# Cross-attention stack on one Trainium2 core: V weight splits, the narrow V and the first head's rows moved in the order of the projection stage

## What is computed

```python
q = x @ Wq; k = ctx @ Wk; v = ctx @ Wv          # 16 heads of 64
logits = einsum('qd,kd->qk', q, k) / 8 + col_bias   # a mask value at 4 named keys
out = softmax(logits) @ v
x = x + concat_heads(out) @ Wo + bo
```

## Time and profile before

| | |
|---|---|
| median of 3 runs | 4579.02 us |
| the profiled execution | 4576.37 us |
| its span, first to last instruction | 4574.6 us |
| granted PE clock, mean | 0.988 of 2.4 GHz |
| PE / DVE / POOL / ACT busy | 98% / 67% / 62% / 50% |
| DMA moved | 349.68 MB, mean 76 GB/s |

### The profile page before, as it was taken

One profiled execution on the slowest core, in us unless ns is written; L12 is line 12 of the kernel. 1 busy time (PEld: TensorE's weight loads), 2 busy tenths in 40 slices (PEclk: granted clock), 3 DMA queues, 4 the chain that ended last, 5 costly groups with the idle time before them and its releaser, 6 DMA issues.

```text
span 4574.6 us, 56775 instructions
## 1 busy us (share of the span) xinstructions
PE 4481.5 (98%) x20609; PEld 2828.0 (62%) x20609; DVE 3081.8 (67%) x5037; ACT 2308.6 (50%) x4121; POOL 2825.7 (62%) x1365
## 2 busy tenths in 40 slices
PE   8999999999999979999999999999999999999999
PEld 7888765656566445555556566656656666666664
DVE  4221567777777678777846777777766677777776
ACT  3232554555455436666655554545555545555553
POOL 0000388889888701011136898889875888898886
PEclk9999999999999979999999999999999999999999
DMA  5474921222221021111243222222126212222220
GB/s 189 156 221 150 305 68 38 66 66 69 48 64 48 13 41 15 13 14 16 57 133 92 64 69 47 66 64 64 41 50 219 63 45 60 63 69 61 51 48 30
DMA packets 124633, 349.68 MB, mean 76 GB/s; under 512 B 28085, under 2 KB 46005, under 8 KB 113338
## 3 DMA queue, kind: packets, MB, share of 16 engines
q1 hardware_dynamic: 124352, 346.04, 28.6%
HBM read 191.31 MB, written 120.31 MB: 68 GB/s over the span
## 4 chain that ended last, share of the span: by engine, by line
PE 93%; DVE 5%; issue 1%; DMA 1%; ACT 0%; SPq 0%; DVEq 0%; ACTq 0%
PE ST L1005 14%; PE SS L986 12%; PE ST L1006 12%; PE OA L1016 12%; PE OB L1016 11%; PE ST L1150 5%; PE OA L1158 4%; PE SS L1136 3%; DVE acc L1612 2%; PE OB L1136 1%; PE SS L1025 1%; PE ST L1081 1%; PE ST L1082 1%; PE ST L1083 1%; PE SS L1052 1%
## 5 line engine op out<-in xcount | busy, mean ns | idle before, releaser
L882 POOL TENSOR_TENSOR acc<-acc,P 128x1024 f32<-128x1024 f32 x912 | 2216.9, 2463 | 298.4 <-DVE acc L1618 285.3
L1346 ACT ACTIVATE P<-ST 128x512 f32<-128x512 f32 (+1 forms) x2496 | 1464.6, 598 | 1254.2 <-PE ST L1006 1128.6
L1591 DVE TENSOR_REDUCE mpart<-SS 128x1 f32<-128x400 f32 (+1 forms) x3072 | 1629.5, 570 | 666.4 <-PE SS L986 590.7
L1005 PE MATMUL ST<-QX,KX 128*128 128x512 f32 (+1 forms) x2496 | 1022.9, 410 | 2.3 <-ACT stw L1244 2.0
L986 PE MATMUL SS<-KS,QS 68*128 68x400 f32 (+1 forms) x3072 | 977.2, 352 | 13.6 <-DMA QS<-stq 8.0
L1006 PE MATMUL ST<-QS,KS 69*128 69x512 f32 (+1 forms) x2496 | 988.4, 396 | 0.0
L986 PEld LDWEIGHTS SS<-KS,QS 68*128 68x128 f32 x3072 | 583.6, 190 | 189.8 <-DVE xacc L1642 24.9
L1005 PEld LDWEIGHTS ST<-QX,KX 128*128 128x128 f32 (+1 forms) x2496 | 463.0, 186 | 359.5 <-issue 271.2
L1016 PE MATMUL OA<-P,Vp 128*64 128x512 f32 (+1 forms) x2496 | 658.3, 606 | 0.0
L1016 PE MATMUL OB<-P,Vp 128*64 128x512 f32 (+1 forms) x2496 | 641.3, 592 | 0.0
L1445 ACT ACTIVATE PG<-ST 128x512 f32<-128x512 f32 (+1 forms) x832 | 426.5, 616 | 215.6 <-PE ST L1150 215.5
(11 more groups left out here) (247 smaller groups left out, 4457.1 us busy)
## 6 DMA issues: line engine op xcount, KB each, us to landing
q_parts<-stq SPq DMA_DIRECT2D x96, 512.0 KB, 5.2
QX<-q_parts SPq DMA_DIRECT2D x96, 512.0 KB, 11.3
KX<-k_parts SPq DMA_DIRECT2D x48, 801.0 KB, 9.4
QS<-q_parts SPq DMA_DIRECT2D x45, 512.0 KB
R<-R SPq DMA_DIRECT2D x360, 64.0 KB, 2.0
v_tiles<-sv SPq DMA_DIRECT2D x24, 832.0 KB, 5.9
Vp<-v_tiles SPq DMA_DIRECT2D x24, 832.0 KB, 7.2
k_parts<-skh SPq DMA_DIRECT2D x48, 400.5 KB, 4.8
```

The costliest lines, as they stand in the source:

```text
L882: gp.tensor_tensor(out, out, P[0:k, slot(H, t), q, :], ALU.add).then_inc(pool_a, 1)
L1005: pe.matmul(bank, KX[H % 2][:, t * 128:t * 128 + k], QX[H % 2][:, q], start=True, stop=False)
L1346: act.activation(P[0:k, slot(H, t), j, :], ST[n % 3][0:k, :], ACT.Exp, scale=SCALE).then_inc(act_p, 1)
L1591: dve.tensor_reduce(mpart[H % 2][:, i // len(KCH), c:c + 1], SS[RING_AT["s", H, i] % 3][:, 0:w], AX.X, ALU.max).then_inc(dve_ss, 1)
```

## The change

Three parts. (1) ACT and DVE split the V weights of an iteration ahead of `take_k` in place of behind `split_wk`; the splits 2 and 3 of the start stand between the two halves of `take_k(0)`. (2) The thirteen transposes of the narrow V (`g`) and their ACT copies go behind the first quad's V, in the bank order too. (3) In SP's last K iteration the first head's K, key rows and bias rows are issued ahead of the last K stores, once PE is through with the last projection, and the four Q copies right behind these stores; the Wq stores, the waits for the landings and the rest of the Q phase follow.

```diff
--- before.py
+++ after.py
@@ -180,9 +180,11 @@
 def before_order():
 
     out = [("c", t, 0) for t in range(KT)]
-    out += [("k", 0, c) for c in range(4)] + [("g", i, 0) for i in range(4)]
+    out += [("k", 0, c) for c in range(4)]
     for qd in range(QUADS):
         out += [("v", qd, t) for t in range(KT)]
+        if qd == 0:
+            out += [("g", i, 0) for i in range(4)]
         if qd == X_QUAD:
             out += [("x", i, 0) for i in range(QT // 2)]
         out += [("k", 1 + 4 * qd + i, c) for i in range(4) for c in range(4)]
@@ -572,6 +574,21 @@
                     sp.wait_ge(dve_wk, m + 3)
                     load_wk(m + 4)
 
+            def load_head_k(H):
+                b, n = H % 3, H // 2
+                sp.dma_start(words(KS[b][0:D, :]), dK[n, H % 2, 0, :, :]).then_inc(d_s[b], 16)
+                sp.dma_start(words(KS[b][D:D + NROWS, :]), dExt[H // HEADS, :, :]).then_inc(d_s[b], 16)
+
+            def load_head_b(H):
+                sp.dma_start(words(QS[H % 3][D:SROWS, :]), dBias.rearrange("m r q -> (m r) q")).then_inc(d_s[H % 3], 16)
+
+            def copy_first_q(l):
+                H0 = l * HEADS
+                for q in range(JQ):
+                    sp.wait_ge(act_qh, QITEMS * l + q + 1)
+                    sp.dma_start(words(QS[H0 % 3][0:D, q * 512:q * 512 + 512]), words(stq[q][0:D, 1, :]))\
+                        .then_inc(d_s[H0 % 3], 16)
+
             store_k(0)
             next_wk(0)
             for qd in range(QUADS):
@@ -586,9 +603,18 @@
                 for w in range(4):
                     sp.dma_start(dV[4 * qd + w, :, :, :], sv[:, w, :, :]).then_inc(d_sv, 16)
                 for i in range(4):
-                    store_k(1 + 4 * qd + i)
-                    next_wk(1 + 4 * qd + i)
                     u, n = 4 * qd + 4 + i, 4 * qd + i
+                    if n + 1 == BIG * PAIRS:
+                        sp.wait_ge(pe_k, 4 * NW)
+                        sp.wait_ge(d_k[1], k_stored(1))
+                        sp.wait_ge(d_ext, 32)
+                        sp.wait_ge(d_bias, 32)
+                        load_head_k(0)
+                        load_head_b(0)
+                    store_k(1 + n)
+                    next_wk(1 + n)
+                    if n + 1 == BIG * PAIRS:
+                        copy_first_q(0)
                     if u + 2 < BIG * PAIRS:
                         sp.wait_ge(dve_wv, u + 1)
                         load_wv(u + 2)
@@ -609,14 +635,6 @@
             for b in range(2):
                 sp.wait_ge(d_wqo[b], 32 * (BIG * PAIRS // 2))
 
-            def load_head_k(H):
-                b, n = H % 3, H // 2
-                sp.dma_start(words(KS[b][0:D, :]), dK[n, H % 2, 0, :, :]).then_inc(d_s[b], 16)
-                sp.dma_start(words(KS[b][D:D + NROWS, :]), dExt[H // HEADS, :, :]).then_inc(d_s[b], 16)
-
-            def load_head_b(H):
-                sp.dma_start(words(QS[H % 3][D:SROWS, :]), dBias.rearrange("m r q -> (m r) q")).then_inc(d_s[H % 3], 16)
-
             def load_head_kx(H):
                 sp.dma_start(words(KX[H % 2][:, :]), dK[H // 2, H % 2, :, :, :].rearrange("r d k -> (r d) k"))\
                     .then_inc(d_x[H % 2], 16)
@@ -656,16 +674,11 @@
 
             def q_phase(l):
                 H0, n0 = l * HEADS, l * PAIRS
-                if l == 0:
-                    load_head_k(0)
-                    load_head_b(0)
                 if l == 2:
                     sp.wait_ge(pe_z, z_banks(H0))
                     load_wq(l, 1)
-                for q in range(JQ):
-                    sp.wait_ge(act_qh, QITEMS * l + q + 1)
-                    sp.dma_start(words(QS[H0 % 3][0:D, q * 512:q * 512 + 512]), words(stq[q][0:D, 1, :]))\
-                        .then_inc(d_s[H0 % 3], 16)
+                if l > 0:
+                    copy_first_q(l)
                 for q in range(QITEMS):
                     n = QITEMS * l + q
                     sp.wait_ge(pool_ql, n + 1)
@@ -952,15 +965,17 @@
                         last = pe.matmul(bank, wkl[b][:, ct, :], ch[:, ct, k], start=False, stop=ct == CCT - 1)
                     last.then_inc(pe_k, 1)
 
+            def transpose_vt():
+                pe.wait_ge(act_k, 4)
+                for i in range(4):
+                    at = BEFORE_AT["g", i, 0]
+                    wait_bank(pe, at)
+                    for t in range(4 * i, min(4 * i + 4, KT)):
+                        k, c = rows_of(t), (t - 4 * i) * 128
+                        last = pe.transpose(PB[at % 8][0:k, c:c + 128], vt[:, t * 128:t * 128 + k], ident[:, :])
+                    last.then_inc(pe_g, 1)
+
             project_k(0)
-            pe.wait_ge(act_k, 4)
-            for i in range(4):
-                at = BEFORE_AT["g", i, 0]
-                wait_bank(pe, at)
-                for t in range(4 * i, min(4 * i + 4, KT)):
-                    k, c = rows_of(t), (t - 4 * i) * 128
-                    last = pe.transpose(PB[at % 8][0:k, c:c + 128], vt[:, t * 128:t * 128 + k], ident[:, :])
-                last.then_inc(pe_g, 1)
             for qd in range(QUADS):
                 pe.wait_ge(dve_wv, 4 * qd + 4)
                 for t in range(KT):
@@ -972,6 +987,8 @@
                         pe.matmul(bank, ch[:, ct, k], wvl[:, ct, :, :], start=False, stop=False)
                         last = pe.matmul(bank, cl[:, ct, k], wvh[:, ct, :, :], start=False, stop=ct == CCT - 1)
                     last.then_inc(pe_v, 1)
+                if qd == 0:
+                    transpose_vt()
                 if qd == X_QUAD:
                     transpose_x()
                 for i in range(4):
@@ -1286,8 +1303,9 @@
                 wait(act, d_wqo[n % 2], 32 * (n // 2))
                 copy(wqs_h[n % 2][:, :, :], wq_raw[n % 2][:, :, :]).then_inc(act_wq, 1)
 
-            def take_k(m):
-                for c, (o, w) in enumerate(KCH):
+            def take_k(m, chunks=range(4)):
+                for c in chunks:
+                    o, w = KCH[c]
                     act.wait_ge(pe_k, 4 * m + c + 1)
                     bank = PB[BEFORE_AT["k", m, c] % 8]
                     if m == 0:
@@ -1299,17 +1317,21 @@
             split_group()
             for u in range(2):
                 split_wv(u)
-            take_k(0)
-            for m in range(2):
-                split_wk(m + 1)
-                split_wv(m + 2)
-            for i in range(4):
-                act.wait_ge(pe_g, i + 1)
-                c = min(4, KT - 4 * i)
-                k = rows_of(4 * i + c - 1)
-                copy(Vg[0:k, 4 * i:4 * i + c, :].rearrange("k t (g d) -> k (t g) d", g=GROUPS)[:, :, 0:D1],
-                     PB[BEFORE_AT["g", i, 0] % 8][0:k, 0:c * 128]
-                     .rearrange("k (t d) -> k t d", d=QD)[:, :, D1:2 * D1]).then_inc(act_g, 1)
+            take_k(0, range(2))
+            for u in range(2, 4):
+                split_wv(u)
+            take_k(0, range(2, 4))
+            for m in range(1, 3):
+                split_wk(m)
+            def take_vg():
+                for i in range(4):
+                    act.wait_ge(pe_g, i + 1)
+                    c = min(4, KT - 4 * i)
+                    k = rows_of(4 * i + c - 1)
+                    copy(Vg[0:k, 4 * i:4 * i + c, :].rearrange("k t (g d) -> k (t g) d", g=GROUPS)[:, :, 0:D1],
+                         PB[BEFORE_AT["g", i, 0] % 8][0:k, 0:c * 128]
+                         .rearrange("k (t d) -> k t d", d=QD)[:, :, D1:2 * D1]).then_inc(act_g, 1)
+
             act.wait_ge(pool_sv, 1)
             for qd in range(QUADS):
                 wait(act, d_sv, 64 * qd)
@@ -1318,15 +1340,17 @@
                     act.wait_ge(pe_v, KT * qd + t + 1)
                     copy(sv[0:k, :, t, :], PB[BEFORE_AT["v", qd, t] % 8][0:k, :].rearrange("k (w d) -> k w d", w=4))\
                         .then_inc(act_v, 1)
+                if qd == 0:
+                    take_vg()
                 if qd == X_QUAD:
                     take_x()
                 for i in range(4):
                     m, u, n = 1 + 4 * qd + i, 4 * qd + 4 + i, 4 * qd + i
+                    if u < BIG * PAIRS:
+                        split_wv(u)
                     take_k(m)
                     if m + 2 < NW:
                         split_wk(m + 2)
-                    if u < BIG * PAIRS:
-                        split_wv(u)
                     split_wq(n)
                     if qd == QUADS - 1:
                         split_x(0, i)
```

## The result

The changed kernel takes 4552.95 us (median of 6 runs, 4547.35 to 4556.11) against 4580.01 (6 runs, 4573.39 to 4583.03): a ratio of 0.9941, interval 0.9929 to 0.9954. The profiled execution took 4553.21, its span is 4551.4, 23.2 us less than before. The forecast was 4557 with a range from 4551 to 4562.

A forecast was written before the change was run, and what follows sets the result against it. The matrix engine, busy nearly the whole span, was taken as the bound, leaving idle and slow-clock time. 18.0 + 2.7 + 1.5 = 22.2 us off 4576.37 gives 4554.2 profiled, median 4556.8, rounded 4557; range 4551 to 4562.

The forecast's parts named there:

- The boundaries: At five K-to-V quad boundaries, earlier V splits remove the wait for narrow V weights: 18.0 us, low end 13.0.
- The narrow V: At the start, V begins 4.2 us earlier, less about 1.5 for thirteen transposes moved behind the first quad: net 2.7 us.
- The condition on the splits: At the start, V splits 2 and 3 must end before 28.3; if not, 1.4 us lost, bounds 1.3 and 2.8.
- The head part in front: Before the first score tile, Q copies land 3.2 us earlier at 121 GB/s; the 8.0 us stall shrinks to about 4.9.
- the bound of 6.0: Before the first score tile, going by SP's issue times alone, the restart comes 6.0 us earlier.
- What takes it back: Before the first score product, a new wait of about 1.5 us for the maxima row; head part nets 1.5 us.
- The risk of half clock: Behind the new maxima-row wait, at the first score product, some risk of half clock; 1.5 to 2.4 us if it came.
- Fast copies: Rival: Q copies fast in a full queue, store stream 3 us earlier, head part 4.7 to 7.1, median 4551 to 4554; chance 0.2.
- The kept stall: Rival: V still waits about 1 us at the boundaries, 18.0 becomes 8 to 13, median 4561 to 4567; chance 0.08.
- the slower case: Rival: late V loads stall ScalarE and some 16 K iterations, 2 us each at 15 us landing, 4607; chance 0.02.

The follow-up runs named there:

- e1: Kernel before plus the V split order alone (start and iterations), narrow V and SP as before: 4556.38 us, ratio 0.9952.
- e2: Kernel before plus only the thirteen narrow-V transposes moved behind the first quad's V: 4581.78 us, ratio 1.0006.
- e4: Kernel before with the four Q copies made twice, all eight waited for: 4581.47 us, one run.
- e5: Changed kernel with the four Q copies made twice behind the last K stores, all eight waited for: 4552.39 us, one run.
- e3: Kernel before plus SP's new order alone: 4575.09 us, ratio 0.9992.
- e9: The changed kernel run again, unaltered: 4552.61 us, ratio 0.9948; its profiled execution took 4561.14.
- e7: Changed kernel with head 0's maxima row issued by ScalarE on its own DMA queue: 4546.36 us, one run.
- e8: Changed kernel with the 2 MB of split Wq loaded one K iteration later: 4556.35 us, one run.
- e11: Changed kernel with head 0's maxima row on ScalarE's queue, timed: 4549.78 us, ratio 0.9939.
- e12: Changed kernel with the four Q copies and head 0's maxima row issued on ScalarE's queue: 4551.38 us, ratio 0.9942.

## Why the prediction was right, point by point

**The boundaries.** Forecast 18.0 us (4.2 three times, 2.7 twice); measured 4.30, 4.12, 2.71, 4.25, 2.72, together 18.10, and e1 alone shows it. V starts 0.18 us behind K at full clock, as taken from the passage to the Q product. The possible 1 or 2 us of ScalarE standing at the moved V load were there, 14.8 us in ten waits over the stage, longest 2.5, and the matrix engine waited for nothing behind them. The 18.0 was read from one execution; in e2 the same boundaries cost 16.7.

**The narrow V.** Forecast 2.7, measured 2.89 in the ledger; the transposes take 1.33 us (64.90 to 66.23) where I had 1.5. The condition on the splits was in the forecast, with its own bounds. What I did not work out is how much of the 2.7 belongs to the split order: e2 alone loses 3 us, and e1 wins 1.6 more than the five boundaries, so the moved transposes add only 1.3.

**The head part in front.** The step "the copies move at 121 GB/s, 0.52 MB in 4.3 us" failed: four more copies cost 2.2 to 2.9 us (e4, e5). Against the last K matmul the restart came 3.4 us earlier in e3 and 4.2 and 5.4 in the two profiles of the changed kernel, in place of 3.2: between my value and the bound of 6.0. The stall left was 2.8 us (4.0 in e3), not 4.9. The half clock behind it, which I took as unchanged, cost 3.4 us in place of 2.5. I had read a rate from a window in which the issues, not the transfers, may have been the limit.

**What takes it back.** The wait for the maxima row was forecast at 1.5 us and was 2.6. The row's landing, forecast about 2 us earlier against the end of K, was 0.9 us earlier in the first profile (66.1 against 67.0) and 2.0 in e9. The mechanism is the one described: it lies in the queue (e7), it comes with the SP order (e3), and since the row's landing stays at 66.1 to 66.2 us behind the last K matmul, it grows when the matrix engine reaches the row sooner (e8) and shrinks when it gets there later (e5). The risk of half clock behind it came true in e3 (1.7 us) and e8, and not in the changed kernel. The net of this part is 1.5 us against e1, 0.9 against before and 0.9 in e3, where 1.5 was booked. That it came out near is luck in part: two terms were off against each other, and the net is about as large as the scatter of K to P, 1.1 us in the changed kernel.

**What was missed.** The first Q product's bank wait (0.8 us, 0.9 in the ledger). ScalarE's wait for a K store behind the 2 MB of Wq was 3.2 us before, without effect; in the first profile it was 6.0, and the first Q product had to wait. e8 shows that the Wq load makes it. Much of the rise is scatter: the same kernel shows 4.1 us and no bank wait in e9, and kernels with the old SP order show 4.2 to 4.4 (e1, e2, e4). Why it lands that late in some executions was not tested.

**The rivals.** "Fast copies" was right in part for the copies and wrong in its result, since the stream behind did not come 3 us earlier. The measured median does lie in that rival's 4551 to 4554 and outside the 4555 to 4558.5 given to the forecast, but the marks show the forecast's mechanism and not the rival's. The kept stall and the slower case did not come. Of the 4 us that the median lies under the point, 1.0 is in the profiled execution (0.6 us less won than forecast at the first score product, 1.6 more behind it, cause not shown). About 3 come from the step to the medians: the profiled execution before lay 2.65 us under the median of its runs, and the one after lies 0.3 over its own, which is scatter.

## What to carry to other kernels

A low part that gates a big stage belongs ahead of the take-overs of results, when nothing waits for these but buffers: reordering two engines' lists won 19.7 us with no instruction changed. Before moving a load to the front of a full queue, look at the last thing in that queue with no slack, here an 8 KB row; here another queue brought it 4 us sooner. And two moves can be worth 2.9 us together where the second alone costs 3.

## What the runs showed of the hardware

The same idle time has no fixed price. Gaps of 2.4 us cost 0.1 or 1.5 us more. A wait of 2.5 us for the maxima row brought the half clock in e3, and one of 2.6 did not in the changed kernel. In e9 a wait of 1.12 us in the last layer came with 0.50, and one of 1.02 in the same place of the first profile with 1.00. Over the whole kernel this made 8 us between two executions of the same program. Small work in a gap may matter: in e2 an idle gap of 4.0 us at the start brought the half clock for 3 us, where the clock stayed at 1.00 in the three profiles with transposes in that gap. The Trainium skill, "TensorE: Matmul & The Clock Gate", Part 1, says that the monitor is free-running against the kernel; these pairs of like waits with a different clock agree with it.

An 8 KB row needed 9.2 us to land behind SP's stores (9.25 in e9) and 5.0 us from ScalarE's queue (4.8 in e11) under the same load. In e12 the issues of the first two copies on that queue took 0.5 us each and those of the next two 2.6 and 2.3, in which ScalarE stood still for 2.0 and 1.3 us. The DMA share was 0.66 and 1.05 at the first two and 0.90 to 1.04 at the others, so the share alone does not tell which; what does was not tested.
